# Layer norm of slot B at other places on all engines of a retention stack, and the work around it moved

## The reference

```python
k, q, v = split(x @ wkqv, 3)
r = tril(q @ k.T / sqrt(d)) / (1 + sqrt(arange(s)))
r = r / clip(abs(r.sum(-1)), 1); r = r @ v          # retention
a, gate = split(r @ w1 + b1, 2)
m = groupnorm1(a * silu(gate) @ w2 + b2)            # moments over the whole sequence
y = m + h
f = gelu(y @ wf1 + bf1) @ wf2 + bf2
h = layernorm(f + y, lg, lb)                        # over the features
```

## Time and profile before

| | us |
|---|---|
| median of three runs | 2443.53 (2442.73 to 2443.81) |
| profiled execution | 2442.89 |
| its span, first to last instruction | 2441.2 |
| PE busy | 2378.8 (97%) |
| DVE, POOL, ACT busy | 1606.4 (66%), 1433.5 (59%), 1341.2 (55%) |
| an iteration inside a layer (start of B's gated projection to the next) | 65.12 |
| granted TensorE clock | 0.995 of full speed |

### The profile page before, as it was taken

How to read it: one execution, slowest core, us unless ns; L and a number is a source line. 1 busy time by engine, 2 the same in 40 slices (tenths; PEclk the granted TensorE clock), 3 DMA queues, 4 the chain that set the end, 5 groups by cost and what they waited for, 6 DMA issues and landing times. The chain is left out here.

```text
span 2441.2 us, 34911 instructions
## 1 busy us (share of the span) xinstructions
PE 2378.8 (97%) x11242; PEld 1968.7 (81%) x11242; DVE 1606.4 (66%) x2953; ACT 1341.2 (55%) x2343; POOL 1433.5 (59%) x1565
## 2 busy tenths in 40 slices
PE   9999999999999999989999999999999999999998
PEld 7888778877888888777888888888888888888886
DVE  3667767667776776678887856665646756565545
ACT  5666666666666666655655544444444444444443
POOL 2345665566655755577987955555645556554444
PEclk9999999999999999999999999999999999999999
DMA  7134454443444344436756554543445433444442
GB/s 250 44 87 103 104 143 100 104 96 99 109 99 97 87 95 100 114 103 208 238 204 211 185 210 160 186 150 137 151 178 185 160 143 138 158 160 168 151 159 74
DMA packets 354870, 344.70 MB, mean 141 GB/s; under 512 B 233872, under 2 KB 319120, under 8 KB 338320
## 3 DMA queue, kind: packets, MB, share of 16 engines
q1 hardware_dynamic: 353728, 341.85, 45.0%
q10 hardware_dynamic: 976, 0.81, 0.1%
HBM read 244.70 MB, written 97.91 MB: 140 GB/s over the span
## 5 line engine op out<-in xcount | busy, mean ns | idle before, releaser
L808 POOL TENSOR_TENSOR hid_lo<-full,hid_hi 128x512 fp32r<-128x512 f32 x384 | 505.4, 1331 | 513.7 <-ACT full L1084 462.2
L1594 DVE SCALAR_TENSOR_TENSOR full<-ps,bias_cols,sum 128x512 f32<-128x512 f32 x384 | 288.1, 750 | 215.7 <-PE ps L1872 196.6
L1870 PE MATMUL ps<-hid_hi,m_w 128*128 128x512 f32 x1024 | 401.8, 392 | 0.1
L1872 PE MATMUL ps<-hid_hi,m_w 128*128 128x512 f32 x1024 | 398.8, 389 | 0.0
L1871 PE MATMUL ps<-hid_lo,m_w 128*128 128x512 f32 x1024 | 398.5, 389 | 0.0
L1081 ACT ACTIVATE hid_hi<-ps,bias_cols 128x512 fp32r<-128x512 f32 x128 | 88.3, 690 | 495.2 <-PE ps L1872 495.2
L1870 PE MATMUL ps<-te_hi,m_w 128*128 128x512 f32 x896 | 351.1, 392 | 1.6 <-DVE sum L1581 1.0
L1872 PE MATMUL ps<-te_hi,m_w 128*128 128x512 f32 x896 | 349.0, 390 | 0.0
L1871 PE MATMUL ps<-te_lo,m_w 128*128 128x512 f32 x896 | 348.7, 389 | 0.0
L1872 PEld LDWEIGHTS ps<-hid_hi,m_w 128*128 128x128 f32 x1024 | 192.2, 188 | 40.3
L1870 PEld LDWEIGHTS ps<-hid_hi,m_w 128*128 128x128 f32 x1024 | 192.3, 188 | 39.6 <-issue 0.5
(11 more groups left out here) (209 smaller groups left out, 5576.5 us busy)
## 6 DMA issues: line engine op xcount, KB each, us to landing
m_w<-prepared SPq DMA_DIRECT2D x96, 1408.0 KB, 6.0
prepared<-m_w SPq DMA_DIRECT2D x32, 1408.0 KB, 5.8
h_store<-h_out SPq DMA_DIRECT2D x32, 512.0 KB, 3.6
we_raw<-in_W SPq DMA_DIRECT2D x64, 256.0 KB, 6.4
gate_bc<-gate_rows SPq DMA_DIRECT2D x64, 256.0 KB, 6.3
z_store<-tmp SPq DMA_DIRECT2D x120, 128.0 KB, 4.0
z<-z_store SPq DMA_DIRECT2D x30, 512.0 KB, 3.9
hT_store<-z SPq DMA_DIRECT2D x96, 128.0 KB, 3.4
```

The source lines that it names most:

```text
L808: nc.gpsimd.tensor_tensor(out=hid_lo[:, k, :], in0=full[:, k, :], in1=f32(hid_hi[:, k, :]), op=ALU.subtract).then_inc(hid_ready, 1)
L1594: nc.vector.scalar_tensor_tensor(out=full[:, k, :], in0=src, scalar=b1_col(e, 2 * fp + BLOCK_ROW[k]), in1=other[:, :], op0=ALU.add, op1=AL ...
L1870: nc.tensor.matmul(out, w[0], x[0], start=first, stop=False, skip_group_check=True)
L1872: return nc.tensor.matmul(out, w[1], x[0], start=False, stop=last, skip_group_check=True)
```

## The change

On DVE, the moments of B's z (of `earlier`) go from the middle of the iteration to its very start, ahead of `residual` of A; the transposes `turn_z` of A go in between the gated products of B, and `turn_h` of A behind them. The moments of A's z go ahead of the gated products of A instead of between them. `residual(B, 0)` goes up between the gated products of A, `residual(B, 1)` from the inside of `groupnorm_out(A)` to ahead of it; in `groupnorm_out(A)` the second sum goes ahead of the first `low_y`. The low halves of B's scores go ahead of `turn_z(B, 1)`, and `turn_h(B)` goes up to follow it directly.

On POOL, the inverse root of B's layer norm goes to the start of the iteration, its gain to ahead of `split_f(B)`, its bias behind it, followed by `split_h(B)`; the masks of B's scores and `split_f(A)` are no longer behind B's gain and bias. On ACT, `normalise_z(B)` goes from the second half of the iteration to behind `high_t(A)`, `high_t(B)` goes ahead of the table load, and at a seam the high half of the vm weights goes up. On PE, the group moments of B go ahead of score block 2 of A, and those of A ahead of the last quarter of the down projection of B half 1. On SP, the store of B's z is issued in two chunks of four DMAs of half the size, each when its `turn_z` is done, and the load of hT for B goes behind `load_z(B)`.

```diff
--- before.py
+++ after.py
@@ -282,7 +282,8 @@
...
         H_STORE = P // BLOCK * DMA
-        Z_STORE, Z_MOVE = P // BLOCK * DMA, (P // BLOCK + 1) * DMA
+        Z_STORE = [n * (P // BLOCK) * DMA for n in (1, DC)]
+        Z_MOVE = [n + DMA for n in Z_STORE]
@@ -526,9 +527,15 @@
...
+            def store_z_chunk(s, it, c):
+                sp.wait_ge(z_ready[s], it * U + residuals(s, c) + 1)
+                for q in range(P // BLOCK):
+                    sp.dma_start(z_blocks[s, q][:, c], turned_z(s)[q * BLOCK:(q + 1) * BLOCK, c, :].rearrange("p (n b) -> p n b", b=BLOCK)
+                                 ).then_inc(z_moved[s], DMA)
+
             def load_z(s, it, turned=True):
-                sp.wait_ge(z_moved[s], it * Z_MOVE + Z_MOVE + Z_STORE)
+                sp.wait_ge(z_moved[s], it * Z_MOVE[s] + Z_MOVE[s] + Z_STORE[s])
                 if turned:
@@ -549,13 +556,14 @@
...
                     load_lnv(B_, lnv_b)
-                store_z(B_, it - 1)
+                for c in range(DC):
+                    store_z_chunk(B_, it - 1, c)
                 if lc_of is not None:
                     load_lc(B_, lc_of)
-                load_T(B_, it + 1)
                 if earlier and turn:
...
                 load_z(B_, it - 1, turn)
+                load_T(B_, it + 1)
                 load(B_, it + 1)
@@ -823,6 +832,8 @@
...
                     split_weight("qk", now.layer)
+                if earlier:
+                    layernorm_rstd(B_, earlier)
                 split_h(A_, now)
@@ -834,11 +845,13 @@
...
                         split_weight("m2", now.layer)
+                    if earlier:
+                        layernorm_gain(pool, nc.gpsimd, B_, earlier, z[B_][:, :, :], BLOCKS)
+                    split_f(B_, before)
+                    layernorm_rstd(A_, before)
+                    if earlier:
+                        layernorm_bias(pool, nc.gpsimd, B_, earlier, z[B_][:, :, :], BLOCKS)
                     split_h(B_, now)
-                    split_f(B_, before)
-                    if earlier:
-                        layernorm_rstd(B_, earlier)
-                    layernorm_rstd(A_, before)
                     if last:
@@ -851,9 +864,6 @@
...
                     split_weight("f2", now.layer)
-                if earlier:
-                    pool.wait_ge(y_ready[A_], now.base + 2)
-                    layernorm_out(pool, nc.gpsimd, B_, earlier)
                 if last:
@@ -1109,11 +1119,13 @@
...
                     gate(B_, before, 1)
+                    if seam:
+                        next_high_weight("vm", now.layer, m_psum[B_], before)
                     high_u(B_, before, 1)
...
                 high_t(A_, now)
-                if seam:
-                    next_high_weight("vm", now.layer, m_psum[B_], before)
+                if earlier:
+                    normalise_z(B_, earlier)
                 if not before:
@@ -1153,14 +1165,12 @@
...
                     next_high_weight("f1", now.layer, f1_psum[B_], before)
+                high_t(B_, now)
                 load_table(ACT.Gelu)
-                high_t(B_, now)
                 if before:
...
                     act.wait_ge(fold_stored, (L - 1) * DMA)
-                if earlier:
-                    normalise_z(B_, earlier)
                 if seam:
@@ -1366,7 +1376,7 @@
...
-            def groupnorm_out(s, at, meanwhile=lambda part: None, between=lambda: None):
+            def groupnorm_out(s, at, meanwhile=lambda part: None):
@@ -1389,13 +1399,17 @@
...
                 summed(0)
-                between()
                 gained(1)
-                meanwhile(0)
-                low_y(s, at, 0)
-                meanwhile(1)
-                dve.wait_ge(gn_done[s], base + 10)
-                summed(1)
+                if s == A_:
+                    dve.wait_ge(gn_done[s], base + 10)
+                    summed(1)
+                    low_y(s, at, 0)
+                else:
+                    meanwhile(0)
+                    low_y(s, at, 0)
+                    meanwhile(1)
+                    dve.wait_ge(gn_done[s], base + 10)
+                    summed(1)
                 low_y(s, at, 1)
@@ -1680,14 +1694,16 @@
...
             def body(now, before, earlier, seam, last=False, turn=True):
+                if earlier:
+                    for blocks in HALVES:
+                        layernorm_stats(B_, earlier, blocks)
+                    layernorm_var(B_, earlier)
                 if before:
...
                         residual(A_, before, c)
-                    for c in range(DC):
-                        turn_z(A_, before, c)
+                    gated_products(B_, before, lambda c: turn_z(A_, before, c))
                     if earlier and turn:
                         turn_h(A_, earlier)
-                    gated_products(B_, before)
                 for c in range(DC):
@@ -1708,17 +1724,16 @@
...
                     sum_moments(0, 0)
-                if earlier:
+                if before:
                     for blocks in HALVES:
-                        layernorm_stats(B_, earlier, blocks)
-                    layernorm_var(B_, earlier)
+                        layernorm_stats(A_, before, blocks)
+                    layernorm_var(A_, before)
+                gated(A_, now, 0)
+                low_u(A_, now, 0)
+                gated(A_, now, 1)
                 if before:
-                    gated_products(A_, now, lambda part: layernorm_stats(A_, before, HALVES[part]))
-                    layernorm_var(A_, before)
                     residual(B_, before, 0)
-                    turn_z(B_, before, 0)
-                else:
-                    gated_products(A_, now)
+                low_u(A_, now, 1)
                 if not before:
@@ -1726,18 +1741,20 @@
...
                 if before:
+                    turn_z(B_, before, 0)
                     groupnorm_in(A_, now)
                     groupnorm_var(A_, now)
-                groupnorm_out(A_, now, between=lambda: before and residual(B_, before, 1))
+                    residual(B_, before, 1)
+                groupnorm_out(A_, now)
+                low_p(B_, now, range(TB))
                 if before:
                     turn_z(B_, before, 1)
-                low_p(B_, now, range(TB))
+                if earlier and turn:
+                    turn_h(B_, earlier)
                 if last:
...
                     low_hT(A_, step_behind(dve, now))
-                if earlier and turn:
-                    turn_h(B_, earlier)
                 for half in range(2):
@@ -2148,10 +2165,10 @@
...
                     fold_vm(0)
-                scores(A_, now, (0, 1, 2), before)
+                scores(A_, now, (0, 1), before)
                 if before:
                     group_moments(B_, before)
-                scores(A_, now, (3,), before)
+                scores(A_, now, (2, 3), before)
                 if not before:
@@ -2177,9 +2194,11 @@
...
                     out_projection(A_, now)
-                    down_projection(B_, before, 1)
+                    down_projection(B_, before, 1, (0, 1, 2))
                 group_moments(A_, now)
-                if not before:
+                if before:
+                    down_projection(B_, before, 1, (3,))
+                else:
                     pe.wait_ge(fold_out, 3 * (L - 1))
```

More of the change, by code:

```diff
@@ L615, in _ @@
                 sp.sem_inc(hT_stored[s], H_STORE)
-                sp.sem_inc(z_moved[s], Z_MOVE)
+                sp.sem_inc(z_moved[s], Z_MOVE[s])
             load_part(0, 0, kq_loaded)
@@ L670, in _ @@
             store_h(B_, STEPS - 3)
-            store_z(B_, STEPS - 2)
+            for c in range(DC):
+                store_z_chunk(B_, STEPS - 2, c)
             load_z(B_, STEPS - 2, False)
@@ L1321, in gated @@
                 if c == 0:
-                    dve.wait_ge(z_moved[s], at.it * Z_MOVE + Z_STORE)
+                    dve.wait_ge(z_moved[s], at.it * Z_MOVE[s] + Z_STORE[s])
                 dve.wait_ge(m_psum[s], at.base + 2 * c + 2)
@@ L1422, in layernorm_stats @@
                 else:
-                    dve.wait_ge(z_moved[s], at.it * Z_MOVE + 2 * Z_MOVE)
+                    dve.wait_ge(z_moved[s], at.it * Z_MOVE[s] + 2 * Z_MOVE[s])
                 for k in blocks:
```

## The result

The changed kernel takes **2405.48 us** (median of four runs, 2404.38 to 2406.31) against 2443.13 before on the same chip: the ratio is 0.9847, with a 95% interval of 0.983 to 0.9864. The forecast was 2409.0, with a range of 2388 to 2434. The profiled execution has a span of 2403.2 us, 38.0 less than before, at a granted TensorE clock of 0.996.

A forecast was written before the change was run, and what follows sets the result against it. PE, 97% busy, with its short waits was taken as the bound. Per iteration −3.6 + 0.2 + 0.8 + 0.4 = −2.2 us; with seams and iterations 1 and 15, −34.8 in all, giving 2409 us, range 2388 to 2434.

The forecast's parts named there:

- the 3.88 us named: PE's time lost per iteration at scores of B, up projection of A and down projection of A half 0, together.
- The 3.6 booked for the second half: Second half of the iteration: gain of 3.6 us booked out of 3.88, the remainder allowed for latencies between engines.
- three losses: PE per iteration: 1.20 us at scores of B, 1.44 at up projection of A, 1.24 at down projection of A.
- +0.2 for low halves of u(A): DVE's low halves of u(A), beside POOL's bias and split_h(B), take 1.2 us instead of 0.69; moments of A come later: +0.2.
- z and its +0.8: Start of iteration: B's z lands late, DVE queues behind it, low halves of u(B) reach the out projection late: 0.7 to 0.8 lost.
- L: Time from the end of turn_z(B, 1) to the landing of B's z: 12.0 us, bounds 11.3 and 17.3.
- S + 9.5: u(B) complete 9.5 us after the iteration's start S, before S + 8.1; PE wants it at S + 8.85.
- The loop L + 50.7: From turn_z(B, 1) to itself: L, 8.55 on DVE, 33.0 on PE, 9.2 to the next; equals 65.12 at L = 14.4.
- slower, 2458: Rival: load of z becomes the bound and is slower; at L = 15.5, +1.1 us in 13 iterations; chance 0.07.
- little change: Rival: z's wait and the gained 3.6 us cancel, L near 14: 2440 us, chance 0.05.
- +0.4 for the moments of B: First half: turn_h(A) delays low_t(A) and group norm statistics of B; PE wants moments of B 0.72 us earlier: +0.4.
- The sum: Ordinary iterations −2.2 us each, seams −2.5 each, iteration 1 −1.7, iteration 15 −3.6: in all −34.8.

The follow-up runs named there:

- the run that has the second half alone: Kernel before, with POOL's gain and bias of B on one of four token blocks, residual(B, 1) early, and DVE's two second-half orders of the changed kernel: 2402.02 us.
- the residual alone: Kernel before, with only residual(B, 1) moved ahead of the group norm's gain of A: 2442.73 us.
- POOL's part out of the way: Kernel before, with POOL doing gain and bias of B on one of four token blocks, the other three left out: 2427.16 us.
- then the residual: Kernel before, with POOL's gain and bias of B on one of four token blocks, plus residual(B, 1) ahead of groupnorm_out(A): 2422.18 us.
- the residual first: Changed kernel, with the residuals of A ahead of the moments of B's z on DVE: 2395.5 us.

## Why the prediction was right, point by point

**The bound.** That PE with its short waits in the second half of the iteration bounds the kernel was right. Of the 3.88 us named, 3.23 are gone in iteration 10.

**The 3.6 booked for the second half** was a little high: 3.23 by the three stages, 3.1 in the run that has the second half alone, and 3.15 from the moments of A to the end of the stage of the down projection, on average over the ten ordinary iterations. What was wrong is that it was booked as three losses, each with its own remedy. The runs show one chain. On the kernel before, the residual alone gives 0.0; POOL's part out of the way 16.1; then the residual 5.0; then DVE's orders 20.2. The largest step came with the one part that the prediction gave no term of its own, the order on DVE ("Following DVE's list from there"); in another sequence of edits the shares would differ. With z on the loop, the same orders are worth only 6.0. The three waits could be added because the change removed all of them at once.

**+0.2 for low halves of u(A)** was not isolated by a run. In the changed kernel they take 1.18 and 1.05 us beside POOL's bias (676.38 and 679.05) where 1.2 was foreseen, and PE's way from the gated projection of A to the moments of A, the three matmuls that moved behind them allowed for, is 0.1 to 0.2 longer in nearly all ordinary iterations.

**z and its +0.8.** The chain was right, nearly row for row, and the price was too high. Foreseen: L = 12.0 from 2.2, 5.8 and 3.9; measured 11.6 from 2.1, 5.6 and 3.9, and up to 12.6 around the seams. z was to land 0.9 behind the start of the iteration; it landed 1.0 behind it in iteration 10 and 0.1 in iteration 11. The next iteration starts 20.9 us behind the moments of A where 20.3 was foreseen: the prediction took all 3.9 us off this way, while it booked 3.6 in its sum, and 3.1 were gone. So z is late only where L is long: the out projection loses 0.6 to 1.0 in iterations 6, 10, 13 and 14, 0.2 in iteration 5 and nothing in the five others, 0.36 on average. u(B) was to be complete at S + 9.5; its last low half ends at 650.73 + 0.69, S + 9.6. A PE wait of 0.5 to 1 was to stand at the out projection; it is 0.65 in iteration 10, but waits on low halves of u are only 9 in all. DVE was to be idle for 2 to 3 us at each iteration's start; it was 0.8 to 1.8, and the prediction's own times (free 0.6 before the start, z 0.9 behind it) give 1.5. By the estimate that the Trainium skill ("DMA: Bandwidth & Descriptors", "Two cost components") allowed, 9.1, z would never have been late. The Trainium skill gives these figures there as a fit to DMAs issued by GpSimd, and SP issues the ones here; for these the trace disagrees, with 11.6 to 12.6. The prediction also said that "everything of the next iteration on DVE is queued behind them", and stopped there; the two residuals needn't be, and that was worth 10 us.

**The loop L + 50.7**, worked out for a rival, is confirmed by three kernels and only in part by a fourth. L + "rest" is the loop by definition; what counts is that the rest, from the landing of z to the next end of `turn_z(B, 1)`, stays near 50.7 while L grows from kernel to kernel. For the nine ordinary iterations at whose start DVE waits for z in these kernels:

| kernel | L | rest | loop, from one such end to the next |
|---|---|---|---|
| changed | 11.6 to 12.6 | 50.0 to 50.9 | 62.3 to 63.5 |
| z stored whole | 13.1 to 14.4 | 50.1 to 50.9 | 63.7 to 65.0 |
| load of hT ahead | 14.2 to 15.7 | 49.9 to 52.0 | 64.8 to 67.1 |
| POOL's gain and bias back | 15.4 to 17.6 | 51.4 to 53.7 | 67.3 to 71.1 |

The changed kernel lies on this loop: the 63.5 of iteration 10 is its L of 12.6, the 62.25 of iteration 11 its L of 11.6. Without it, the second half alone allows 62.02. The prediction named L = 14.4 as the point from which the loop decides, by comparing with 65.12; but that is where the kernel becomes no faster than before. By these runs the loop binds from about 62.0 − 50.7 = 11.3 on. The rival "slower, 2458" had the right mechanism, and the fourth row is the case in which it comes true. But its rule doesn't give the size: L is 16.7 there on average and the rest 52.4, so some 1.7 us more of each iteration lie outside L. That 3.1 us (the 17.5 of iteration 10 over 14.4) in 13 iterations would give 2483, where 2482.34 was measured, is chance. The third row is "little change", reached by a single line of SP's order.

**+0.4 for the moments of B.** The cost was right: the scores of A with these moments take 4.39 us instead of 3.98 in iteration 11, and 4.43 in iteration 10. Only the wait that the list shows is smaller than the 0.3 to 0.5 foreseen: 0.15 to 0.20 each, in 9 of the row's 14 waits (its long ones, 0.8 to 0.9, are those of the moments of A at the seams). The rest is matmuls that start late without showing as idle. But this cost hangs on the late DVE and not on the place of the moments: with the residual first it is gone. And the place itself pays: put back, the kernel is 3.2 slower. The prediction left out what the earlier moments give to the retention of A and the up projection of B behind them: −0.23 on average.

**The sum.** Ordinary iterations −2.34 on average (−2.2 foreseen), seams −2.8 (−2.5), iteration 1 −2.2 (−1.7), iteration 15 −3.1 (−3.6), together with 0.7 in iteration 0 38.0 against 34.8. By the stages of the ten ordinary iterations, −2.34 is −3.15 for the second half (−3.6 booked), +0.36 for z (+0.8), +0.38 for the moments of B (+0.4), +0.15 for u(A) (+0.2), −0.23 at the retention of A and the up projection of B (not booked), and +0.14 that lies at the end of iteration 7 alone, just ahead of a seam. So the close sum is partly luck: the second half was booked 0.45 too high as a gain, and z 0.44 too high as a cost.

## What to carry to other kernels

When several waits of the bounding engine end at the same chain, each one's length in the trace is not its price: removing one of them may give nothing, and the same edit is worth something once the others are gone. Walk the chain, and look for the operation that stands in the list ahead of the one that is waited for. When a load moves onto the critical loop, follow the issuing queue backwards: what counts is what stands ahead of it in the list and what that waits for, not its bytes; and put work that needs no load ahead of the instruction that waits for it.

## What was not expected of the hardware

- A load of 0.41 us issue time ahead of four stores cost 37 us in a run of 2405, some 2.4 in each iteration. SP issued in order: the load was issued at 654.68, when DVE had done with its buffer at 654.65, and the stores only behind it, from 655.27.
- The issue of four DMAs with half the bytes each took 1.93 to 2.05 us in nearly all rows of the changed kernel that show four of them alone, that of four whole ones 2.94 to 3.06 (its slot A, and most of those of the kernel with z stored whole): about a third less, not half. Of the 1.6 us by which L is shorter with chunks, 1.05 are theirs (2.14 against 3.19 from the end of the transpose to the next issue), 0.43 the hT stores and their wait behind them (5.64 against 6.07), 0.1 the load.
- DVE's operations on two SBUF operands took 1.22 us beside POOL's gain instead of 0.69 to 0.75, three in a row. One piece of POOL's gain takes 3.72/4 = 0.93 there and 2.81/4 = 0.70 for slot A, with DVE elsewhere. The Trainium skill ("SBUF — State Buffer", "SBUF: two separate sides") says that of such a pair the one that starts first locks the other out for its whole instruction. The rows fit that on DVE's side: 0.53 more is less than one piece of POOL. They don't fit a DVE that stops until POOL is through with all four. Whether the two take turns or both run slower at the same time, no row here can tell.
